# A decoder layer on one core: indicator products of 256 columns, more short products of ones, and a new order in the first four periods

## The reference, cut to what matters

```python
x = _layernorm(x + mamba2(x))      # H=16 heads, ch=16, N=64, per sequence of T=1024, B=4
x = _layernorm(x + cross_attention(x, ctx, mask))
x = _layernorm(x + relu(x @ W1 + b1) @ W2 + b2)
# mamba2, per head:
logA = einsum('hoc,bthc->btho', W_logA, x) + b_logA
X, Bm, Cm = split(silu(einsum('hoc,bthc->btho', W_XBC, x) + b_XBC))
cum = cumsum(logA); A_ss = where(causal, exp(cum_i - cum_j), 0)
Y = einsum('bhij,bjhc->bihc', A_ss * (Cm . Bm), X)
out = (gate * Y) @ W_out.T + b_out
```

## Time and profile before

| | |
|---|---|
| median of 3 runs | 671.2 us (670.6 to 674.76) |
| the profiled execution | 671.81 us |
| its span, first to last instruction | 670.1 us |
| mean granted TensorE clock | 0.98 |
| busy PE / DVE / POOL / ACT | 632.9 / 553.6 / 469.1 / 455.1 us |
| products of ones (L540) | 48, from 1.1 to 80.0 us |
| indicator products (L340) | 56, from 21.5 to 592.2 us |

### The profile page before, as it was taken

The page is one execution under the profiler, slowest core; times in us unless marked ns, Lnnn a source line. Parts: engine busy times, 40 slices in busy tenths (PEclk is TensorE's granted clock), DMA queues, the critical chain, the costliest instruction groups (busy, mean ns, idle before and its releaser), DMA issues.

```text
span 670.1 us, 22057 instructions
## 1 busy us (share of the span) xinstructions
PE 632.9 (94%) x8342; PEld 542.3 (81%) x8342; DVE 553.6 (83%) x1335; ACT 455.1 (68%) x1115; POOL 469.1 (70%) x756
## 2 busy tenths in 40 slices
PE   6989988889999999999999999999999999999897
PEld 4667766668888888888888888888888888899786
DVE  2367778888899898989899898889889898898764
ACT  3967657677778686868678686868678686433332
POOL 1342666667878687787868687787869687879563
PEclk7799998889999999999999999999999999999999
DMA  3422455444344444545345443445345453634201
GB/s 111 175 52 45 119 119 149 118 128 124 97 121 128 128 119 101 127 127 133 110 121 146 110 136 81 129 138 132 101 124 148 104 138 97 158 96 119 48 17 32
DMA packets 86950, 75.54 MB, mean 113 GB/s; under 512 B 44989, under 2 KB 81725, under 8 KB 86845
## 3 DMA queue, kind: packets, MB, share of 16 engines
q1 hardware_dynamic: 86429, 73.85, 41.2%
q10 hardware_dynamic: 416, 0.28, 0.1%
HBM read 41.53 MB, written 31.72 MB: 109 GB/s over the span
## 4 chain that ended last, share of the span: by engine, by line
PE 74%; DVE 12%; ACT 6%; issue 3%; DMA 2%; POOL 1%; SPq 1%; ACTq 0%; POOLq 0%; DVEq 0%
PE bank L520 12%; PE bank L532 11%; PE bank L365 9%; PE bank L309 5%; PE bank L426 4%; PE bank L499 4%; PE bank L468 4%; PE bank L379 3%; PE bank L509 2%; PE bank L486 2%; PE bank L293 2%; PE bank L352 2%; PE bank L321 2%; PE bank L540 2%; PE bank L393 2%
## 5 line engine op out<-in xcount | busy, mean ns | idle before, releaser
L1115 DVE TENSOR_TENSOR E<-bank,E 128x512 f32<-128x512 f32 x128 | 81.8, 680 | 21.2 <-PE bank L365 17.5
L1503 POOL TENSOR_TENSOR P<-P,rc 128x308 f32<-128x308 f32 x120 | 80.8, 700 | 21.0 <-DVE rc L1276 20.9
L1463 POOL TENSOR_SCALAR_AFFINE_SELECT E<-E 128x508 f32<-128x508 f32 x128 | 80.3, 651 | 0.0
L365 PE MATMUL bank<-Cc,Bc 64*128 64x128 f32 x1024 | 72.6, 287 | 3.7 <-DVE cmat L1098 2.7
L818 ACT ACTIVATE E<-bank 128x512 f32<-128x512 f32 x128 | 68.0, 599 | 10.9 <-PE bank L352 10.6
L365 PEld LDWEIGHTS bank<-Cc,Bc 64*128 64x128 f32 x1024 | 63.2, 192 | 14.4 <-issue 5.6
L532 PE MATMUL bank<-w2h,hh 128*128 128x256 f32 x256 | 74.5, 291 | 0.0
L1527 POOL TENSOR_TENSOR hl<-hr,hh 128x512 fp32r<-128x512 f32 x56 | 72.1, 1297 | 0.3
L532 PE MATMUL bank<-w2l,hh 128*128 128x256 f32 x256 | 71.7, 280 | 0.0
L532 PE MATMUL bank<-w2h,hl 128*128 128x256 f32 x256 | 71.7, 280 | 0.0
L897 ACT ACTIVATE hr<-bank,cst 128x256 f32<-128x256 f32 x128 | 54.7, 495 | 18.6 <-PE bank L520 16.7
(11 more groups left out here) (126 smaller groups left out, 1795.5 us busy)
## 6 DMA issues: line engine op xcount, KB each, us to landing
turn_p<-TP SPq DMA_DIRECT2D x120, 160.0 KB, 2.8
PT<-turn_p SPq DMA_DIRECT2D x30, 640.0 KB, 4.2
xr<-in_x SPq DMA_DIRECT2D x32, 128.0 KB, 2.5
out<-res SPq DMA_DIRECT2D x32, 128.0 KB, 2.8
xT<-in_xT SPq DMA_DIRECT2D x15, 256.0 KB, 3.1
turn_x<-xr SPq DMA_DIRECT2D x120, 32.0 KB, 1.8
tT<-turn_x SPq DMA_DIRECT2D x30, 128.0 KB, 2.7
turn_x<-x SPq DMA_DIRECT2D x120, 32.0 KB, 2.0
```

Source lines behind the costliest of these rows:

```text
L365: i = eng.matmul(b_g[n, u, r][:, 128 * q:128 * q + 128], Bc[k, g % 2, 2 * q + u, cols(n)], Cc[k, g % 2, 2 * q + u, cols(n)], start=True, s ...
L1115: eng.tensor_tensor(E[:, h % 4, r, :, :], b_g[n, u, r][:, :].rearrange("p (h t) -> p h t", h=4), E[:, h % 4, r, :, :], ALU.mult).then_inc( ...
L1463: eng.affine_select(out=E[:, h % 4, r, :, 0:127], in_=E[:, h % 4, r, :, 0:127], compare_op=ALU.is_ge, fill=0.0, base=0, pattern=[[0, 4], [ ...
L1503: eng.tensor_tensor(v, v, rc[:, n % 2, 4 * j:4 * j + 4].unsqueeze(2).to_broadcast([128, 4, S]), ALU.mult).then_inc(p_norm, 1)
```

## The change

The two indicator products of `ecum` read `DL` through a step of zero twice over, so that each has 256 columns and writes half a bank; the exponential reads the first 128 columns of each half. `warm` is 14 products for k=0 and 4 for all others, and is called 16 times instead of 6. Two waits are added for the turned tiles at the end (`x1_turn`, `x2_turn`). The order of the first four periods is new on all five engines; the loop from s=4 on is the same on TensorE, VectorE, ScalarE, GpSimd and SyncE.

```diff
@@ TensorE, ecum
-                    i = eng.matmul(bk[:, 128 * h:128 * h + 128], ind[:, h, :], DL[:, n % 2, :], start=True, stop=True)
+                    i = eng.matmul(bk[:, 256 * h:256 * h + 256], ind[:, h, :],
+                                   DL[:, n % 2, :].unsqueeze(1).to_broadcast([128, 2, 128]), start=True, stop=True)
@@ TensorE, x1_turn and x2_turn
+                pe.wait_ge(x1_flip, n)
...
+                pe.wait_ge(x2_flip, n)
@@ TensorE, warm
-                for _ in range(8):
+                for _ in range(14 if k == 0 else 4):
@@ TensorE, the first calls of the order
             warm(0)
+            warm(1)
             tok(0)
             tok(1)
+            warm(2)
             cum(0)
+            cum(1)
             bc(0, 0)
-            cum(1)
+            tok(2)
             bc(0, 1)
-            tok(2)
...
@@ ScalarE, ecum
-                eng.activation(ec[:, n % 2, :], b_ec[n][:, 0:256], ACT.Exp).then_inc(ec_exp, 1)
+                eng.activation(ec[:, n % 2, :].rearrange("p (h t) -> p h t", h=2),
+                               b_ec[n][:, :].rearrange("p (h t) -> p h t", h=2)[:, :, 0:128], ACT.Exp).then_inc(ec_exp, 1)
@@ GpSimd, the order
             decay(0, 0)
             decay(0, 1)
+            split_w(0)
             x_resid(0)
             decay(1, 0)
+            decay(1, 1)
             ln1_rstd(0)
-            decay(1, 1)
-            split_w(0)
             x_resid(1)
+            split_w(1)
+            x_resid(2)
             decay(2, 0)
...
```

More of the change, by code:

```diff
@@ L566, in _ @@
             warm(0)
+            warm(1)
             tok(0)
             tok(1)
+            warm(2)
             cum(0)
+            cum(1)
             bc(0, 0)
-            cum(1)
+            tok(2)
             bc(0, 1)
-            tok(2)
+            ecum(1)
+            warm(3)
             diff(0, 0)
-            ecum(1)
-            warm(1)
             diff(0, 1)
+            warm(4)
+            warm(5)
             gmat(0, 0)
+            gmat(0, 1)
+            warm(6)
             diff(1, 0)
+            cum(2)
             diff(1, 1)
-            gmat(0, 1)
-            cum(2)
             state_in(0)
+            y(0)
             bc(1, 0)
-            y(0)
+            ecum(2)
             gate(0)
+            gmat(1, 0)
+            warm(7)
             out_proj(0)
             tok(3)
+            state_turn(0)
+            gmat(1, 1)
+            state_in(1)
+            cum(3)
             bc(1, 1)
-            gmat(1, 0)
-            state_turn(0)
+            warm(8)
+            warm(9)
+            inter(1)
+            ecum(3)
             keys()
-            state_in(1)
             tok(4)
-            diff(2, 0)
[L596 to L601, removed]
+            y(1)
+            gate(1)
+            bc(2, 0)
+            state_turn(1)
+            values()
+            diff(2, 0)
+            cum(4)
             diff(2, 1)
-            bc(2, 0)
-            gate(1)
-            y(1)
+            diff(3, 0)
+            out_proj(1)
             query(0)
[L607 to L612, removed]
             inter(2)
-            warm(2)
             gmat(2, 0)
@@ L617, in _ @@
             gmat(2, 1)
-            tok(5)
[L619 to L622, removed]
+            state_in(2)
+            state_turn(2)
+            warm(10)
+            score(0)
+            gate(2)
+            ecum(4)
+            warm(11)
+            y(2)
+            warm(12)
+            diff(4, 0)
+            warm(13)
+            gmat(3, 0)
+            tok(5)
+            out_proj(2)
+            bc(2, 1)
+            gmat(3, 1)
+            cum(5)
+            tok(6)
+            state_in(3)
             query(1)
-            bc(2, 1)
+            warm(14)
             score(1)
[L626 to L633, removed]
             diff(4, 1)
-            gmat(3, 1)
+            gmat(4, 0)
             state_turn(3)
-            tok(6)
+            y(3)
             inter(3)
-            y(3)
             gate(3)
-            gmat(4, 0)
+            warm(15)
+            cum(6)
+            out_proj(3)
             bc(3, 0)
-            out_proj(3)
-            cum(6)
             inter(4)
@@ L902, in _ @@
             cum_top(0)
+            cum_top(1)
             bc(0, 0)
-            cum_top(1)
+            tok(2)
             bc(0, 1)
-            tok(2)
             ecum(1)
@@ L1584, in _ @@
             ln1_rstd(5)
+            u_rest(0)
             x_resid(6)
-            split_w(3)
-            x1_bias(4)
-            u_rest(0)
             for s in range(4, 16):
@@ L1833, in _ @@
             get_x1(3)
+            load_resid(5)
             get_p(1)
-            load_resid(5)
-            load_x(4)
             put_x2(0)
-            load_w(3)
-            rows(6)
             for s in range(4, 17):
```

159 lines of the change are left out of this document (81 added, 78 removed).

## The result

The changed kernel takes **676.75 us** (median of 14 runs, 674.41 to 679.34). The kernel before took 672.53 us on the same chip (14 runs, 670.6 to 676.6). The ratio is **1.0057, 95% interval [1.0034, 1.008]**: a small loss, but the interval lies above 1. The forecast was 673.2 with a range from 664 to 681. The time is inside it, but 3.5 us above the likeliest value, and several of the steps towards that value were off.

The account below looks back on a forecast made before the run. TensorE was taken to bound the kernel from about 145 us, a chain over all engines before. Profiled 671.8 + 2.0 (products) + 0 (start) = 673.8, stated as a median of 673.2 us; range 664 to 681.

Parts of the forecast that it names:

- What bounds the kernel: TensorE sets the pace from about 145 us on; before that, a chain over all engines.
- The end of the start: Up to `pv(0)`: copies' issues end near 92, `diff(5, 0)` +1.3 us, some 1.5 us back; start in all about 0.
- The products' term, +2.0 us: `ecum`'s 28 pairs of indicator products, widened to 256 columns: +0.07 us a pair, +2.0 us in all.
- the pair therefore costs 0.17 us, 0.085 each: Narrow pair's cost, from the same place (L509 to L352) with and without it; wide pair put at 0.24 us.
- The narrow products are dearer than they look: Faster rival on `ecum`'s products: widening saves 5.9 us instead of costing 2.0, total 665.3; chance 0.06.
- Full clock from 7.81: Start on TensorE: eighteen ones last to about 6.8 us, leaving 1 us idle, so full clock is expected from 7.81.
- `y(0)` near 27.6: Tile 0's products with the decay matrix (L379) start near 27.6 instead of 30.67, a lead of 3.1 us.
- `out_proj(0)` near 33.4: Start on TensorE: `out_proj(0)` waits behind ScalarE and `warm(7)`, near 33.4 where it had 33.19; the lead is gone.
- ready near 81: Tile 0's probabilities turned near 81; the value copies queued behind them end issuing near 92 and land near 94.
- Some 1.5 us come back: DMA queue at `put_x2(0)`: the weight load and row copies just behind it move earlier, returning some 1.5 us.
- `x_resid(2)` ahead of `decay(2, 0)`: GpSimd: it waits for a load near 56 while the exponential is ready near 54; 2 us lost on tile 2 alone.
- The DMA queue and GpSimd hold up tiles 2 to 4: Slower rival: loads and row copies strung behind `split_w(1)` and `x_resid(2)`, +6 us, 681 with the products; chance 0.25.

Follow-up runs that it names:

- the mended new order: Changed kernel with all value copies issued early, `x_resid(5)` later on GpSimd and ten ones in the bank of `bc(0, 1)`: 674.4 us, ratio 1.0025.

## Why the prediction was right, and where its steps were not

- **What bounds the kernel: right.** The stretch after 153 us kept its pace, and the loss lies in the start, as "The end of the start" had it.
- **The products' term, +2.0 us: sign right, size off.** The step that failed is "the pair therefore costs 0.17 us, 0.085 each". It took the pair out of a place where part of it lies under its neighbours. In a stream a narrow product costs 0.11, the spacing of two loads of its weight; a wide one 0.12, which the 0.24 for the pair had right. The difference is 0.02 for a pair, and 28 of them give 0.5 us. With a single pair the timeline of after shows +0.05 at the place of the earlier trace rows:

```profile
230.77 1.03 PE L512 MATMUL bank<-w,oT 128*128 128x256 f32 x4
231.44 0.58 PE L340 MATMUL bank<-DL,ind 128*128 128x256 f32 x2
231.95 0.51 PE L353 MATMUL bank<-RB,DL 10*128 10x512 f32 x4
```

  L512 to L353 is 1.18 where it was 1.13. Ahead of the second feed-forward product the pair takes 0.43 instead of 0.36, but the first gap behind it is 0.12 instead of 0.17, +0.02 in all. From `pv(4)` to `pv(27)` the whole drift is 0.52 us. (The 2.3 us of the earlier trace rows are the largest sum, not the longest wait; it changes nothing.) The Trainium skill ("TensorE: Matmul & The Clock Gate", Back-to-back issue gap) gives 262 cycles for the wide product, by that an estimate of 0.109 us, where the stream shows 0.12. Its 134 cycles for 128 columns, on which the +3.0 was built, are what it calls the isolated gap of a single product, and this stream with a new weight each time shows 0.11. The same page of the Trainium skill (section LDWEIGHTS) has P / 1.2 ns for a load of P columns, an estimate of 107 ns for 128 columns, and the 0.11 between two loads agrees with that.
- **"The narrow products are dearer than they look": half right.** They are, 0.22 for a pair and not 0.17, but not 0.45, and the wide ones are no cheaper.
- **Full clock from 7.81: right for 9 us only.** The step that failed is "`y(0)` near 27.6". I filled the first gap (more than filled it: the eighteen products lasted to 8.08, not 6.8) and did not look for the next: TensorE waits 2.52 us ahead of the second `bc`, and the clock is at half for 10.2 us. `y(0)` came at 31.57. With ten more ones it came at 28.71, so the arithmetic of the step was fair and the missing wait was its fault.
- **`out_proj(0)` near 33.4: wrong, 38.33.** The links were the ones named (`ecum(2)` ahead of `bc(1, 0)` on ScalarE, `warm(7)` on the bank that the first Silu frees; its wait of 1.51 shows above). They start from a `y(0)` 4 us later. Even with the clock held it was 35.44, so the chain was 2 us short as well. That the lead would be gone by here came true, but by the fall of the clock at 17 us as well as by these links.
- **The probabilities of tile 0 "ready near 81", the copies' end "near 92", `pv(0)` near 94, `diff(5, 0)` near 97: wrong, and this is the step that mattered.** The sum behind it is 11.2 us of issues (it has nine copies, though the sentence ahead of it speaks of the last six of before). In after the issues from `put_p(0)` to the last copy take 12.3 us, 85.97 to 98.29. So 1.1 us is the sum, and 5.0 is its start: VectorE had turned these probabilities only at 85.95. Behind the copies stand eight row copies, and `diff(5, 0)` came at 103.30. `pv(0)` at 100.39 lies behind the 99 that I had named as the sign of a wrong link. But what held `pv(0)` was not the copies: it is as late with them early (100.36), because `gmat(4, 1)` ahead of it waits for VectorE. The copies act behind it, on `diff(5, 0)` and on the load for `x_resid(5)`. The kernel lost 0.57%, 3.8 us, of which the products are about 0.5: the start cost about 3 us by the ratio instead of 0. Moving the copies brought 2.7 us in the profile and 4 by the ratios, give or take 2.3 (1.0057 to 0.9998).
- **"Some 1.5 us come back" with `put_x2(0)`:** nothing of it is to be seen. That issue (L1779, L1765 before) starts at 114.75 where it was at 106.00, and what lies behind the eight row copies at 106.84 is `put_x1(3)`.
- **`x_resid(2)` ahead of `decay(2, 0)`, 2 us on tile 2:** it was waited for until 59.8 and cost nothing to be seen. The same pattern did stand on the chain, at `x_resid(5)`, where I had not looked; moving it gave 0.2%, within the uncertainty.
- **The rivals.** The slower one ("The DMA queue and GpSimd hold up tiles 2 to 4") named the right engine and the wrong place. The split of the weights ended at 46.21 (43.79 and 2.42), and `rows(2)` went out from 46.66 where I had it at about 41 to 44, but `diff(2, 0)` didn't start before 57.85 and no wait for these copies stands ahead of it. The queue held tile 5 and the values instead. Its +6 was nearer the truth than my 0, and the products' smaller price made up for a part. The forecast of the total was near for a reason that is partly luck: a term 1.5 too dear and, between the medians, a start 3.7 too cheap. Another 1.3 us of the distance to 676.75 is that the kernel before had its median at 672.53 in the larger set, where I had 671.2.
- **What stays open:** the copies are shown to be a part of the loss. How much the stretches at half clock and VectorE's lag add in the new order is not separated.

## What to carry to other kernels

An issue queue is a chain like an engine: when a change moves issues, write down every issue of the queue with its duration from the first one that waits, and look for what is ready behind it. In this kernel, ready copies behind waiting issues cost 2.7 us in the profile and about 4 by the ratios, and moving them forward brought the new order back to the time of before and made the old one 0.5% faster. Price a narrow product by its spacing in a stream, not by taking one pair out of its surroundings. And before two profiles are compared, lay their stretches at half clock side by side: a difference of 3 us in the start can be an edit or another fall of the clock, and only a pair in which these stretches agree, or many runs, tells them apart.

## What the runs showed that I had not expected

- A product of 128 columns with a new weight of 128 rows and 128 columns each time costs 0.11 us where one of 256 costs 0.12. For such products doubling the columns is nearly free.
- In the start the clock fell behind idle times of TensorE, and where the first was filled it fell later: at 7.8 in before, at 11.0 with 17 ones, at 17.0 in after behind 2.52 us, and not before 58 with ten ones in that place. It isn't the same in every execution: the wait ahead of the token block was 2.26 to 3.08 us in the three profiles of the old order with 8 ones in which the clock fell at 7.8 to 8.8, and 1.21 and 1.79 in the two where it stayed full beyond 55. Filling the second gap brought `out_proj(0)` 2.9 us and the kernel nothing that could be measured, since the clock fell elsewhere.
- The share of time at the full clock differs between executions of one kernel, and in the new order the time goes with it: the mended new order took 670.09 at a mean granted clock of 0.999 and 678.46 at 0.986; the changed kernel 675.4 to 675.8 at 0.996 and 679.3 at 0.984. Before doesn't follow such a line: it took 669.91 at 0.992 and 671.77 at 0.977, but also 676.04 at 0.991. A single profile of such a kernel can be 3 us from its median, as after's is.
